# Masks ahead of scores, the second expert layer between halves of the first, and another order of the opening

## The chip, the cores and the metric

One core of a Trainium2 chip runs the kernel in one launch. The metric is the device time of that launch in microseconds (us). Three runs of the kernel before took 550.11, 551.80 and 550.82 us, median 550.82.

## The reference

A pre-norm block on x of 16 batches x 256 tokens x 128 features, all float32:

```python
x = x + attention(layernorm(x))   # 16 heads, d_k 8, d_v 64, causal softmax, then @ Wo
x = x + experts(layernorm(x))
# experts: probs = softmax(h @ gate_w) over 8 experts; each expert of each batch takes
# its top 64 of 256 tokens (top_k over tokens), y = gelu(xin @ w1) @ w2 with 512 hidden
# features, y *= top_p, and y is added back at the tokens' places
```

## The kernel before

**Attention.** Four heads of one batch are a unit `u = 4*b + j`; 64 units follow one another, and each engine runs the same software pipeline over them (`batches` calls `batch` per engine: batches -2 to 3 and 10 to 15 written out, the others in a hardware loop). All order is that of the instructions on each engine, with semaphores between engines. In one step, TensorE (PE) does: the second block's scores of unit u+1 into `s1_ps` (queries 128 to 255 against all 256 keys), the contexts of u-2 (L1075), once per batch extra work (transposed norms L1206, queries and keys L1034 to L1036, gate L1092), the transposes of the probabilities of u-1 (L1048, L1049), the output projection of u-3 (L1084), the last transposes (L1058), the values of u+2 (L1034 to L1036) and the first block's scores of u+2 into `s0_ps` (L1276). ScalarE (ACT) does the exponentials (L529) and half of the copies out of PSUM, VectorE (DVE) the row maxima (L939, L883), the other copies and the norms, GpSimd (POOL) the multiplication of the probabilities by their inverse sums (L482, L489). SyncE (SP) issues the transfers.

`s1_ps` is two banks, two heads in each. The scores are two matmuls on 64 rows of the array each (L1189, rows 0 to 63 for heads 0 and 1, rows 64 to 127 for heads 2 and 3; the queries are held as high and low parts in float32r, and 32 rows belong to a head). The causal mask is added by the array: four matmuls of bfloat16 tiles of 64 rows, 64 query columns by two heads (L1194). The whole step waits for `exp1`, the end of the exponentials of the block that the banks held before. A semaphore `s1_done` after the last of the six matmuls releases the row maximum.

**Opening.** `batch` with b = -2 and -1 fills the pipeline. There ACT clears the eight parts of the two key tiles (`zero_keys`, L522), four of them ahead of the first copy of transposed norms (L600); queries and keys are stored to DRAM and read back in the layout of the scores (SP L300, L328, L331), and the first unit's scores wait for that.

**Experts.** For n = 0 to 15, `n // 4` is a quarter of the batches and `n % 4` a pair of experts. PE runs `hidden(n, 0)` to `hidden(n, 3)` (L1146 to L1148, six matmuls of 256 columns each, 24 in all), `expert_out(n-1)` (L1162, 64 matmuls of 64 weight columns) and `out_product(n-5)` (L1172, eight matmuls, which put the rows of batch n-5 back at their tokens). `hidden` has two halves of a bank pair, `h_ps[k % 2]`: `hidden(n, k)` waits until ACT's gelu (L577) has read half k-2. `gather(b)` (L1125, four matmuls) fetches the tokens of batch b for the experts; `GATHERED_AT` and `GATHERED_AFTER` say at which n. ACT's `copy_xin` and DVE's `split_xin` turn it into `xin_hi` and `xin_lo`. DVE also builds the selection tiles (`picks` L830, `placing` L853), scales y (`scale_y` L875), finds the top tokens of batches 8 to 15 in 23 rounds (`top_round`, L790 to L796; one DMA round trip by `store_toks` and `load_toks` follows them) and adds the results (`add_out` L861, L864). y goes from L875 to ACT's L587 and POOL's L506, whose `y_lo_ready` `out_product` waits for.

## Time and profile before

| what | us |
|---|---|
| median of 3 runs | 550.82 |
| lowest, highest | 550.11, 551.80 |
| the profiled execution, its own time | 549.33 |
| its span in the trace | 547.60 |
| PE busy in the span | 517.3 (94%) |
| PE weight loads busy | 425.8 (78%) |
| DVE, ACT, POOL busy | 415.6, 405.0, 253.7 |
| mean granted clock of PE | 0.991 |

A matmul row begins when the matmul enters the array, and its length holds its way through the array too, so rows of one engine overlap; what a matmul costs is the distance from its start to the start of the next. PEld rows are the weight loads. The name after "<-" in brackets is what ended an engine's idle time.

### The profile page before, as it was taken

The numbers are of one execution on the slowest core, as the hardware profiler recorded it, in microseconds if no ns is written. First come the engines' busy times: TensorE is split into PE (matmuls) and PEld (weight loads), VectorE is DVE, ScalarE is ACT, GpSimd is POOL, SyncE is SP. The second block draws the span as 40 slices with busy tenths as digits, with TensorE's granted clock in tenths as the row PEclk, the third lists the DMA queues.
The fourth block names the chain that finished last, engine by engine and source line by source line (L and its number), as shares of the span: only waits on it lengthen the run. The fifth ranks groups of instructions, "written<-read, shape, count | busy, mean of one in ns | idle before, by whom it ended". The sixth has DMA issues, their size and how long they took to land.

```text
span 547.6 us, 13959 instructions
## 1 busy us (share of the span) xinstructions
PE 517.3 (94%) x4777; PEld 425.8 (78%) x4777; DVE 415.6 (76%) x1066; ACT 405.0 (74%) x1383; POOL 253.7 (46%) x249
## 2 busy tenths in 40 slices
PE   1489999999999999999999999999999999999996
PEld 1257777878878778787787877867789989899995
DVE  1477888888888888888999999999954876443354
ACT  4699999889998899988989889899555443424320
POOL 5165566565655655556555665556900110111011
PEclk9979999999999999999999999999999999999999
DMA  4576252742633325142251422502200012000011
GB/s 125 153 189 160 78 153 54 238 115 61 170 110 107 87 66 153 41 112 78 78 156 34 123 79 76 155 1 76 76 7 1 2 46 63 11 22 11 11 30 50
DMA packets 49783, 45.97 MB, mean 84 GB/s; under 512 B 4288, under 2 KB 46528, under 8 KB 49728
## 3 DMA queue, kind: packets, MB, share of 16 engines
q1 hardware_dynamic: 48864, 44.60, 29.9%
q8 instruction: 32, 0.52, 0.4%
q10 hardware_dynamic: 864, 0.66, 0.4%
q14 instruction: 23, 0.19, 0.1%
HBM read 26.35 MB, written 18.89 MB: 83 GB/s over the span
## 4 chain that ended last, share of the span: by engine, by line
PE 89%; ACT 4%; DVE 4%; issue 1%; DMA 1%; ACTq 0%; POOL 0%; DVEq 0%
PE ctx_ps L1075 16%; PE t_ps L1162 11%; PE misc_ps L1084 10%; PE t_ps L1048 5%; PE t_ps L1049 5%; PE s_ps L1189 5%; PE t_ps L1058 5%; PE misc_ps L1034 4%; PE s_ps L1146 4%; PE misc_ps L1036 3%; PE misc_ps L1035 3%; PE s_ps L1147 3%; PE s_ps L1148 3%; PE s_ps L1276 2%; PE ctx_ps L1172 2%; ACT prob L529 2%
## 5 line engine op out<-in xcount | busy, mean ns | idle before, releaser
L529 ACT ACTIVATE prob<-s_ps,neg_max 128x128 f32<-128x128 f32 (+1 forms) x512 | 208.4, 426 | 3.7 <-DVE neg_max L939 1.7
L489 POOL TENSOR_TENSOR probn<-prob,inv 128x1024 f32<-128x1024 f32 x64 | 121.2, 1893 | 54.7 <-DVE inv L960 54.7
L529 ACT ACTIVATION_READ_ACCUMULATOR prob<-s_ps,neg_max 128x1 f32 x512 | 108.4, 212 | 0.0
L482 POOL TENSOR_TENSOR probn<-prob,inv 128x512 f32<-128x512 f32 x64 | 66.6, 1040 | 67.3 <-PE t_ps L1058 59.0
L883 DVE TENSOR_REDUCE neg_max<-s_ps 128x4 f32<-128x1024 f32 x64 | 76.3, 1193 | 0.9 <-PE s_ps L1194 0.8
L506 POOL TENSOR_TENSOR y_parts<-y_sb,y_parts 128x512 fp32r<-128x512 f32 x16 | 20.6, 1286 | 112.7 <-ACT y_parts L587 112.7
L577 ACT ACTIVATE hT<-s_ps 128x512 f32<-128x512 f32 x64 | 38.0, 596 | 44.7 <-PE s_ps L1148 42.2
L1084 PE MATMUL misc_ps<-wo_sb,ctxT 128*128 128x128 f32 x512 | 67.8, 275 | 0.8 <-DVE x_all L708 0.8
L1084 PEld LDWEIGHTS misc_ps<-wo_sb,ctxT 128*128 128x128 f32 x512 | 62.2, 192 | 1.2 <-issue 1.2
L1048 PE MATMUL t_ps<-ident,probn 128*128 128x128 f32 x256 | 61.8, 281 | 0.0
L1049 PE MATMUL t_ps<-ident,probn 128*128 128x128 f32 x256 | 60.1, 275 | 0.0
L939 DVE TENSOR_REDUCE neg_max<-s_ps 128x4 f32<-128x512 f32 x64 | 44.2, 690 | 16.7 <-PE s_ps L1276 15.8
L538 ACT ACTIVATE probT<-t_ps 128x512 f32<-128x512 f32 x64 | 38.2, 597 | 18.9 <-PE t_ps L1049 18.0
L753 DVE COPY probT<-t_ps 128x512 f32<-128x512 f32 x64 | 44.1, 689 | 8.1 <-PE t_ps L1058 6.3
L1075 PE MATMUL ctx_ps<-probT,v_odd 128*64 128x256 f32 (+1 forms) x512 | 48.7, 332 | 0.8 <-ACT probT L543 0.7
L1075 PE MATMUL ctx_ps<-probT,v_even 128*64 128x256 f32 (+1 forms) x512 | 48.7, 332 | 0.7 <-DVE probT L753 0.5
L747 DVE COPY ctxT<-ctx_ps 128x512 f32<-128x512 f32 x64 | 43.5, 680 | 0.1
L1075 PEld LDWEIGHTS ctx_ps<-probT,v_odd 128*64 128x64 f32 x512 | 32.1, 136 | 14.0 <-ACT probT L543 1.2
L1075 PEld LDWEIGHTS ctx_ps<-probT,v_even 128*64 128x64 f32 x512 | 32.3, 136 | 13.0 <-issue 1.3
L892 DVE CAST s_ps<-causal 128x512 f32<-128x512 bf16 x63 | 42.4, 672 | 0.0
L1048 PEld LDWEIGHTS t_ps<-ident,probn 128*128 128x128 f32 x256 | 37.1, 145 | 3.9 <-issue 3.8
L543 ACT ACTIVATE probT<-t_ps 128x512 f32<-128x512 f32 x64 | 39.7, 620 | 0.0
(176 smaller groups left out, 1158.9 us busy)
## 6 DMA issues: line engine op xcount, KB each, us to landing
qT<-q_rows SPq DMA_DIRECT2D x15, 512.0 KB, 4.0
q_rows<-qk_hi SPq DMA_DIRECT2D x32, 128.0 KB, 2.4
q_rows<-qk_lo SPq DMA_DIRECT2D x32, 128.0 KB, 2.4
k_diag_odd<-k_rows SPq DMA_DIRECT2D x32, 128.0 KB, 4.2
k_rows<-qk_hi SPq DMA_DIRECT2D x30, 128.0 KB, 2.4
k_rows<-qk_lo SPq DMA_DIRECT2D x30, 128.0 KB, 2.4
k_diag_even<-k_rows SPq DMA_DIRECT2D x28, 128.0 KB, 4.2
w_raw<-in_L_ffn_w SPq DMA_DIRECT2D x1, 2048.0 KB, 9.8
```

Of the source, the lines that this page charges most:

```text
L482: nc.gpsimd.tensor_tensor(probn[r][:, 0:HG * P].rearrange("p (i k) -> p i k", i=HG), prob[r][:, 0:HG * P].rearrange("p (i k) -> p i k", i=HG),
L489: nc.gpsimd.tensor_tensor(probn[r][:, HG * P:].rearrange("p (i k) -> p i k", i=HG), prob[r][:, HG * P:].rearrange("p (i k) -> p i k", i=HG ...
L529: last = nc.scalar.activation(prob[r][:, first + i * keys:first + (i + 1) * keys], scores[:, i, :], ACT.Exp, bias=neg_max[:, r, block_, i: ...
L747: nc.vector.tensor_copy(ctxT[r][:, :, :], ctx_ps[:, :, :]).then_inc(ctx_ready, 1)
L753: nc.vector.tensor_copy(probT[rm][:, 1024:1536], t_ps[rm][:, :]).then_inc(t_dve, 1)
L883: nc.vector.tensor_reduce(out=neg_max[:, r1, 1, :], in_=s1_ps[:, :, :], axis=AX.X, op=ALU.max, negate=True).then_inc(max1, 1)
L939: nc.vector.tensor_reduce(out=neg_max[:, r2, 0, :], in_=s0_ps[:, :, :], axis=AX.X, op=ALU.max, negate=True).then_inc(max0, 1)
L1048: nc.tensor.transpose(t[:, i, 0:P], q0[:, 2 * f + i, :], ident[:, :])
L1049: last = nc.tensor.transpose(t[:, i, P:T], q1[:, 2 * f + i, 0:P], ident[:, :])
L1075: last = nc.tensor.matmul(ctx_ps[half * DV:(half + 1) * DV, pair, kb * P:T], v_sb[vb][:, kb, h * DV:(h + 1) * DV], rhs, start=(kb == 0), s ...
L1084: last = nc.tensor.matmul(misc_ps[1][:, tb * D:(tb + 1) * D], ctxT[r][:, c, tb * P:(tb + 1) * P], wo_sb[:, 2 * g + c, :], start=(g == 0 an ...
L1162: last = nc.tensor.matmul(y_ps[half * CAP:(half + 1) * CAP, q, :], hT[m % RING][:, half, c, q * CAP:(q + 1) * CAP], w2_of(2 * (m % EP) + h ...
```

## The change

1. `second_scores` puts the four mask matmuls ahead of the two score matmuls; the masks start the accumulation and the scores end it. The waits are the same.
2. In the expert stage PE runs `hidden(n, 0)`, `hidden(n, 1)`, `expert_out(n-1)`, `hidden(n, 2)`, `hidden(n, 3)`, then gathers, then `out_product(n-5)`, for each n. Batches 8 and 9 are gathered amid n = 7 in place of after n = 6. The gate product of batch 15 moves from the end of n = 1 into n = 2. DVE's work is reordered to go with it: the top rounds are split into parts ahead of and behind `scale_y` (`TOPS_AHEAD`, `TOPS_BEHIND`), `slots(1)` moves from n = 5 to n = 7, and the placing tiles of batches 12 to 15 lie in `xin_hi[0]` and `xin_lo[0]` (free once `hidden(11, 3)` is done) and are built at n = 12 to 15.
3. At the end `out_product` of batches 14 and 15 is done whole after the last y is ready; batches 12 and 13 still have three of four pairs ahead of it.
4. The opening is written out by hand for each engine, and the loop starts at b = 0. ACT clears two parts of the first key tile, after the first copy of transposed norms, and DVE the other six; the first norm comes ahead of the split of the weights; POOL computes both scales ahead of the mask tiles; two of the four first key loads are issued by ACT; both value products of the first tokens come ahead of the first scores.

```diff
-GATHERED_AFTER = {6: (8, 9), 7: (10, 11)}
+GATHERED_AMID = {7: (8, 9)}
+GATHERED_AFTER = {7: (10, 11)}
+TOPS_AHEAD = {4: range(6, 10), 5: range(15, 23)}
+TOPS_BEHIND = {3: range(0, 6), 4: range(10, 15)}
+LAST_PLACES_AT = 12
...
+            def second_scores(q, kb):
+                tiles = ((slice(0, HALF), 0), (slice(HALF, P), 2))
+                for half in range(2):
+                    cols = slice(P + half * HALF, P + (half + 1) * HALF)
+                    for rows, i in tiles:
+                        nc.tensor.matmul(s1_ps[:, i:i + 2, cols], half_rows[rows, half, :],
+                                         bcast(half_masks[rows, half, :], 1, 2),
+                                         start=(half == 0), stop=False, skip_group_check=True)
+                for rows, i in tiles:
+                    last = nc.tensor.matmul(s1_ps[:, i:i + 2, :], qT[kb][rows, q, P:T], k_diag[kb][rows, q, i:i + 2, :],
+                                            start=False, stop=True, skip_group_check=True)
+                last.then_inc(s1_done, 1)
...
+                for b in GATHERED_AMID.get(n, ()):
+                    gather(b)
+                if n == 2:
+                    pe.wait_ge(x2T_ready, B)
+                    gate(B - 1, side_ps)
+                if has(n - 1, B):
+                    expert_out(n - 1)
+                if has(n, B):
                     hidden(n, 2)
                     hidden(n, 3)
...
-            for b in range(LAST, B):
+            for b in range(LAST, B - 2):
                 out_product(b, range(EP - 1))
             pe.wait_ge(y_lo_ready, B)
-            for b in range(LAST, B):
+            for b in range(LAST, B - 2):
                 out_product(b, [EP - 1]).then_inc(out_done, 1)
+            for b in range(B - 2, B):
+                out_product(b, range(EP)).then_inc(out_done, 1)
```

The openings of ACT, DVE and PE in turn, which take the place of `batch` with b = -2 and -1:

```diff
+            split_norms(0, 0)
+            zero_keys(0, range(2))
+            split_qk(0)
+            act.wait_ge(qk_hi_done, 1)
+            store_rows(act, qk_hi, K_HI)
+            act.wait_ge(qk_lo_done, 1)
+            store_rows(act, qk_lo, K_LO)
+            act.wait_ge(wv_loaded, 16)
+            nc.scalar.activation(wv_hi[:, :], wv_raw[:, :], ACT.Copy).then_inc(w_hi, 1)
+            split_norms(1, 1)
+            act.wait_ge(qk_stored, QK_STORES)
+            act.wait_ge(zeroed, 3)
+            for i in range(2, HG):
+                act.dma_start(f32(k_diag[0][i * ROWS:(i + 1) * ROWS, 0:1, i, :]),
+                              k_rows.rearrange("(j i) r d t -> i (r d) j t", j=G)[i][:, 0:1, :]).then_inc(first_loaded, 16)
+            copy_values(0, 0, 0)
+            copy_values(1, 1, 0)
+            act.wait_ge(max0, 1)
+            exps(0, 0, s0_ps, P, 0, exp0)
+            split_qk(1)
+            act.wait_ge(max1, 1)
+            exps(0, 1, s1_ps, T, HG * P, exp1)
...
+            dve.wait_ge(x_loaded[0], 16)
+            norm_stats(lambda tb: x_all[:, tb, :], bn6, mv1, bn1_done, 1, stats1)
+            norm1(0)
+            split_qk_weights()
+            dve.wait_ge(x_loaded[1], 16)
+            norm_stats(lambda tb: x_all[:, TB + tb, :], bn6, mv1, bn1_done, 2, stats1)
+            split_norms(0, 0)
+            zero_keys(0, 2)
+            split_qk(0)
+            zero_keys(0, 3)
+            norm1(1)
+            zero_keys(1, 0)
+            dve.wait_ge(w_hi, 3)
+            nc.vector.tensor_tensor(wv_lo[:, :], wv_raw[:, :], f32(wv_hi[:, :]), ALU.subtract).then_inc(w_lo, 1)
+            split_norms(1, 1)
+            for j in range(1, G):
+                zero_keys(1, j)
+            dve.wait_ge(s0_done, 1)
+            nc.vector.tensor_reduce(out=neg_max[:, 0, 0, :], in_=s0_ps[:, :, :], axis=AX.X, op=ALU.max, negate=True).then_inc(max0, 1)
+            dve.wait_ge(s1_done, 1)
+            nc.vector.tensor_reduce(out=neg_max[:, 0, 1, :], in_=s1_ps[:, :, :], axis=AX.X, op=ALU.max, negate=True).then_inc(max1, 1)
+            dve.wait_ge(exp0, 1)
+            nc.vector.reciprocal(inv[:, 0, 0, :], sums[:, 0, 0, :]).then_inc(inv0, 1)
+            nc.vector.tensor_copy(s0_ps[:, :, :], bcast(causal[:, :], 1, HG)).then_inc(filled0, 1)
+            split_qk(1)
+            dve.wait_ge(s0_done, 2)
+            nc.vector.tensor_reduce(out=neg_max[:, 1, 0, :], in_=s0_ps[:, :, :], axis=AX.X, op=ALU.max, negate=True).then_inc(max0, 1)
+            dve.wait_ge(exp1, 1)
+            nc.vector.reciprocal(inv[:, 0, 1, :], sums[:, 0, 1, :]).then_inc(inv1, 1)
...
+            turn_first_norms(0)
+            pe.wait_ge(w_hi, 2)
+            pe.wait_ge(w_lo, 2)
+            pe.wait_ge(xT_ready, 1)
+            queries_keys(0)
+            nc.tensor.matmul(s0_ps[:, :, :], ident_bf[:, :], bcast(causal[:, :], 1, HG), start=True, stop=True)
+            pe.wait_ge(qk_lo_done, 1)
+            turn_first_norms(1)
+            pe.wait_ge(w_hi, 3)
+            pe.wait_ge(w_lo, 3)
+            pe.wait_ge(xT_ready, 2)
+            values(0, 0)
+            pe.wait_ge(v_ready, 1)
+            values(1, 0)
+            pe.wait_ge(v_ready, 2)
+            pe.wait_ge(first_loaded, QK_LOADS)
+            first_scores(0, 0)
+            pe.wait_ge(halves, 10)
+            second_scores(0, 0)
+            queries_keys(1)
+            pe.wait_ge(qk_loaded, QK_LOADS)
+            pe.wait_ge(filled0, 1)
+            first_scores(1, 0)
+            pe.wait_ge(qk_lo_done, 2)
```

## Rows read from the trace of the kernel before

**Rows 1.** The page: the chain that ended last, by engine.

```profile
PE 89%; ACT 4%; DVE 4%; issue 1%; DMA 1%; ACTq 0%; POOL 0%; DVEq 0%
```

**Rows 2.** Windows: span of window, busy us of each engine, granted clock, DMA.

```profile
30.00:35.00 5.00, 3.78 (x14) 1.96 (x14) 3.89 (x12) 4.90 (x24) 3.88 (x5) 0.50 0.50 142
...
100.00:200.00 100.00, 99.82 (x871) 79.84 (x870) 87.24 (x216) 90.77 (x348) 58.81 (x51) 1.00 0.45 127
```

**Rows 3.** Timeline, opening: start us, us, engine, line, operation.

```profile
6.59 3.87 ACT L522 ACTIVATE k_diag_even<-eps_sb 128x1024 fp32r<-128x1024 f32 x4
7.17 0.59 DVE L692 TENSOR_SCALAR xn<-x_all,mv,rstd 128x128 f32<-128x128 f32 x2
...
10.37 0.36 ACT L600 ACTIVATE xT_hi<-misc_ps 128x256 fp32r<-128x256 f32 x1
...
12.99 0.60 ACT L604 ACTIVATE qk_hi<-misc_ps 128x512 fp32r<-128x512 f32 x1 [2.26 <-PE misc_ps L1036]
...
19.23 0.35 SPq L328 DMA_DIRECT2D qT<-q_rows  x1
...
21.40 0.76 PE L1034 MATMUL misc_ps<-wv_hi,xT_hi 128*128 128x512 f32 x1 [1.02 <-DVE xT_lo L920]
...
28.99 0.49 PE L1189 MATMUL s_ps<-k_diag_even,qT 64*128 64x512 f32 x2
```

**Rows 4.** Timeline, two attention steps, PE and the exponential before each.

```profile
201.67 0.22 ACT L529 ACTIVATION_READ_ACCUMULATOR prob<-s_ps,neg_max 128x1 f32 x1
201.73 0.40 PE L1276 MATMUL s_ps<-k_diag_even,qT 128*128 128x512 f32 x1
...
202.06 0.49 PE L1189 MATMUL s_ps<-k_diag_even,qT 64*128 64x512 f32 x2
...
202.40 0.28 PE L1194 MATMUL s_ps<-half_masks,half_rows 64*128 64x128 bf16 x4
...
202.61 1.52 PE L1075 MATMUL ctx_ps<-probT,v_odd 128*64 128x256 f32 x16
...
207.83 0.23 ACT L529 ACTIVATION_READ_ACCUMULATOR prob<-s_ps,neg_max 128x1 f32 x1
...
208.11 0.50 PE L1189 MATMUL s_ps<-k_diag_even,qT 64*128 64x512 f32 x2
```

**Rows 5.** Timeline, first unit: a bfloat16 matmul, then a float32r one.

```profile
22.90 0.61 PE L1275 MATMUL s_ps<-causal,ident_bf 128*128 128x512 bf16 x1
22.91 0.31 PEld L1276 LDWEIGHTS s_ps<-k_diag_even,qT 128*128 128x128 f32 x1
...
23.87 0.79 PE L1189 MATMUL s_ps<-k_diag_even,qT 64*128 64x512 f32 x2
```

**Rows 6.** Waits: engine, line, waited for: us in total, times, longest.

```profile
PEld s_ps L1189 <- ACT prob L529: 23.2, 61, 0.7
```

**Rows 7.** Timeline, one turn of the expert stage on PE.

```profile
521.61 3.71 PE L1162 MATMUL t_ps<-w_first,hT 128*64 128x128 f32 x64
525.26 0.39 PE L1146 MATMUL s_ps<-xin_hi,w_hi 128*128 128x256 f32 x1
...
526.68 0.28 PE L1148 MATMUL s_ps<-xin_hi,w_lo 128*128 128x256 f32 x1
526.99 0.39 PE L1146 MATMUL s_ps<-xin_hi,w_hi 128*128 128x256 f32 x1
...
528.52 1.12 PE L1172 MATMUL ctx_ps<-y_parts,place 128*128 128x256 f32 x8
529.57 3.71 PE L1162 MATMUL t_ps<-w_rest,hT 128*64 128x128 f32 x64
```

**Rows 8.** Timeline, the end: last products, last addition.

```profile
538.01 0.98 PE L1172 MATMUL misc_ps<-y_parts,place 128*128 128x256 f32 x6
...
544.33 0.42 DVE L864 TENSOR_TENSOR x_all<-misc_ps,x_all 128x256 f32<-128x256 f32 x1
```

**Rows 9.** One line: count, min/median/max ns of one, first and last start.

```profile
L790 DVE MAX8 top<-left x16: 407/420/422, 289.2 to 441.7; 64x8 f32<-64x256 f32 x16
```

More of the change, by code:

```diff
@@ L188, in block_kernel @@
                                   t_ps[0][:, :], misc_ps[1][:, :])]
-        last_place = [part[:, :, :].rearrange("p t (a n) -> p (t a) n", a=2) for part in pick]
+        last_place = [half for part in (xin_hi[0], xin_lo[0]) for half in
+                      (part[:, 0:EP, :, :].rearrange("p e q s -> p e (q s)"),
+                       part[:, EP:E, :, :].rearrange("p e q s -> p e (q s)"))]
         def w2_of(e):
@@ L302, in batches @@
         def batches(engine, batch):
-            for b in range(-2, 4):
+            for b in range(4):
                 batch(b, b % 2)
@@ L517, in _, with zero_keys @@
                                      scale=(DK ** -0.5 if w == 0 else 1.0)).then_inc(w_hi, 1)
-            def zero_keys(r):
+            def zero_keys(r, groups):
                 act.wait_ge(consts, 4)
-                for j in range(G):
+                for j in groups:
                     last = nc.scalar.activation(k_diag[r][:, j, :, :].rearrange("p i t -> p (i t)"),
@@ L841, in split_xin, with take_gathered @@
                                         f32(xin_hi[b // QB % RING][:, :, b % QB, :]), ALU.subtract).then_inc(xin_lo_ready, 1)
+            def take_gathered(b):
+                if b + 1 not in (PASS, PASS + 3, PASS + 4) and b + 1 < B:
+                    picks(b + 1)
+                split_xin(b)
             def placing(b):
@@ L980, in _ @@
             for n in range(B + 2):
+                for b in GATHERED_AT.get(n, ()):
+                    take_gathered(b)
                 if n == 1:
@@ L1020, in _ @@
                     scale_y(m)
-                if n == 5:
+                if n == 1:
+                    copy_x2T(B - 1, side_ps)
+                if n == 3:
+                    copy_probs(1, side_ps[0:HALF, 0:T])
+                for s in TOPS_BEHIND.get(n, ()):
+                    top_round(1, s)
+                if n == 7:
+                    picks(PASS + 4)
+                for b in GATHERED_AFTER.get(n, ()):
+                    take_gathered(b)
+                if n == 6:
+                    picks(PASS)
                     picks(PASS + 1)
+                    placing(2)
                 b = n - 5
-                if has(b, LAST) and b % QB == 0:
+                if has(b, LAST):
                     add_out(b)
+                b = {4: -1, 5: 1}.get(n, n - 3)
+                if has(b, LAST):
+                    await_count(dve, out_done, b - 1)
+                    placing(b)
             for b in range(LAST, B):
@@ L1182, in batch @@
                     if has(u + 1, UNITS):
-                        q, kb = (j + 1) % G, par if j < 3 else 1 - par
-                        if isinstance(u, int) and u == -1:
-                            pe.wait_ge(halves, 10)
                         await_count(pe, exp1, u + 1)
-                        tiles = ((slice(0, HALF), 0), (slice(HALF, P), 2))
-                        for rows, i in tiles:
-                            nc.tensor.matmul(s1_ps[:, i:i + 2, :], qT[kb][rows, q, P:T], k_diag[kb][rows, q, i:i + 2, :],
-                                             start=True, stop=False, skip_group_check=True)
-                        for half in range(2):
-                            cols = slice(P + half * HALF, P + (half + 1) * HALF)
-                            for rows, i in tiles:
-                                last = nc.tensor.matmul(s1_ps[:, i:i + 2, cols], half_rows[rows, half, :],
-                                                        bcast(half_masks[rows, half, :], 1, 2),
-                                                        start=False, stop=(half == 1), skip_group_check=True)
-                        last.then_inc(s1_done, 1)
+                        second_scores((j + 1) % G, par if j < 3 else 1 - par)
                     if has(u - 2, UNITS):
@@ L1317, in _ @@
                     gather(b)
+                if n == 6:
+                    turn_tops(1)
                 if n == 3:
@@ L1324, in _ @@
                     turn_norms(B - 1, side_ps)
-                b, m = n - 5, n - 1
-                if b % QB == 0 and has(m, B):
-                    expert_out(m)
+                b = n - 5
                 if has(b, LAST):
@@ L1334, in _ @@
                     out_product(b, range(EP)).then_inc(out_done, 1)
-                if b % QB != 0 and has(m, B):
-                    expert_out(m)
-                if n == 1:
-                    pe.wait_ge(x2T_ready, B)
-                    gate(B - 1, side_ps)
-                if n == 5:
-                    turn_tops(1)
             pe.wait_ge(xin_hi_ready, B)
```

192 lines of the change are left out of this document (88 added, 104 removed).

## The prediction

> **What bounds the kernel now.** I read the page first. In its chain that ended last PE holds 89% and every other engine 4% or less [rows 1]: time taken from PE comes off the end. The windows then say where: from 100 to 200 us PE is busy for 99.82 of 100 us at a granted clock of 1.00, while DVE and ACT have 87.24 and 90.77 [rows 2]. But a busy PE row holds the way through the array, so the third view is the timeline of PE in one step, where the distance between starts is the cost. There three places show where PE gives time away: the opening, the switch to the second block's scores, and the break between the halves of the first expert layer. The change touches all three.
>
> **Opening.** It isn't PE-bound: a chain of single operations leads to the second unit's scores at 28.99 [rows 3]. The copy of the transposed norms starts at 10.37, since ACT has four clearings ahead of it (6.59 to 10.46), although the norm is written from 7.17 on [rows 3]. What follows hangs on it at fixed distances: queries and keys copied at 12.99, first key load issued at 19.23 (after the stores have landed), values at 21.40, first scores behind the masks at 22.90 [rows 3, 5].
> After the change the norm starts without waiting for the split of the weights, about 5.5 by my estimate, and ACT's copy follows at about 6.9. DVE then computes the second batch's statistics before it splits the norms, to about 8.5; PE's six matmuls start at 8.6, and ACT's copy of queries and keys at about 10.15 in place of 12.99: 2.85 us earlier. The two clearings left on ACT (3.87 / 4 = 0.97 each) lie under this. The stores and key loads keep their distance of 6.2 us (12.99 to 19.23): issue at 16.4, and two of the four issues go to ACT, so the keys are there at about 19.5.
> Now the values are late next: ACT issues its four stores, then splits the value weights (about 13.4 to 14.5), DVE splits them to 15.7 behind one clearing, and PE starts the values at 16.3. Two products, each followed by ACT's copy and a wait for it (21.40 + 0.76 for the first matmul of one, about 2.2 with its copy), end at 20.8. First scores then, against 22.95: 2.1 us earlier, and as ACT's exponentials of the first block no longer stand behind a late second block, I get the scores at 28.99 at about 26.1. DVE's six clearings cost 1.1 us each (my estimate; ACT's are 0.97), and four of them stand behind the first stores, where DVE waits anyway. POOL's mask tiles end about 4 us later, at 14.6, well before their first use at 21.4. I take 2.9 us. Bounds: the copy at 12.99 moves by at most 12.99 - 6.69 - 2.6 = 3.7; and 0.5 if DVE's clearings or the two value products take the place of what went. The clock comes in here: the trace has 0.50 (1.2 GHz) in the window 30 to 35 after a stretch with gaps [rows 2], and whether it still falls there moves about 1 us either way.
>
> **Masks ahead of scores.** 64 times; 60 of them where PE is the bound. The page's waits put 23.2 us of PE's weight loads before L1189 down to ACT's exponentials [rows 6], 0.37 each. The timeline corrects that: the last exponential ends at 201.67 + 0.22 = 201.89, and L1189 starts at 202.06, 0.17 later; at 208.11 it starts 0.05 after 207.83 + 0.23 [rows 4]. So 0.05 is what the semaphore needs, and in most steps something else sets the start: L1276 to L1189 is 0.33, where 512 columns at 2.4 GHz are 0.213. About 0.11 goes to the change from 128 rows to 64. The order of masks and scores doesn't touch that.
> What it touches is the 0.55 from 202.06 to 202.61. The score matmuls' rows are 0.49 long against 0.40 for L1276 [rows 4]: 0.095 of exposed weight load. So before: 0.095 load, 0.213 columns, 0.03 to the masks at 202.40, 0.12 for four masks of 128 columns, two at a time, and 0.09 to turn the array to L1075. The masks' own loads are bfloat16 and short (none of it visible before 202.40).
> After: masks first, 0.01 of load and 0.12 of columns. The score loads can start when the second pair of masks streams, at +0.08, and need 0.095: scores at +0.17, end of columns at +0.39, contexts at +0.48. Saved: 0.07 per unit, 60 x 0.07 = 4.2 us.
> For this the float32r load has to run under a bfloat16 matmul. Rows 5 show that it does: the load of L1276 starts at 22.91, 0.01 after the bfloat16 matmul L1275, and from 22.90 to 23.87 there are 0.97 us, which is two times 512 columns at 1.2 GHz (0.853) and the 0.11 of the turn: nothing is left for an exposed load. That is with 128 rows, though; in the masked tiles no row shows it. Bounds for the step: no overlap, 0.00 (load 0.095 still exposed, now between masks and scores); full overlap, 0.095 + 0.03 = 0.125, or 7.5 us. Below nothing: if each change between mask pairs and scores also drained the array at 0.11, two of them would make it 0.55 + 0.20. I take 0.07, nearest to rows 5 with the shorter cover of 128 columns.
> The Trainium skill speaks against me here: its page "TensorE: Matmul & The Clock Gate", section "Part 3: Packing small matmuls — row/col tiling", says that a weight load overlaps running matmuls only when it goes to another row group; the scores' loads go to the masks' own row groups. By it the step saves nothing (rival 1).
> Who follows? ACT's chain of a step starts from PE's transposes, so it moves along. Where ACT is busy from one step to the next, its slack before L1189 is 0.17 - 0.05 = 0.12 [rows 4], more than 0.07. s1_done comes 0.07 earlier too. In the last four units DVE sets the pace; they give nothing and are left out.
>
> **Expert stage.** One turn of n before: L1162 521.61 to 529.57 = 7.96 [rows 7]. In it the second half of `hidden` starts at 526.99, 0.31 after the last matmul at 526.68, where the spacing is 0.12: 0.19 of waiting for gelu; and its first matmul is 0.39 long against 0.28, 0.10 of exposed load: 0.29 in all. With L1162 (3.65) between the halves, gelu (0.6) is hidden. The array is still turned twice per n, once into L1162 and once out, as before. And `hidden(n+1, 0)` now follows `out_product`, whose 0.96 covers the gelu that it needs (it ends 0.2 + 0.6 after half 2, and half 3 alone takes 0.72). So 0.29 to 0.30 for each n from 5 to 15, and 0.1 more at n = 5, 9 and 13, where the old order put L1162 next to L1172 and cost a turn: 11 x 0.295 + 0.3 = 3.5. For n = 1 to 4 there is no `out_product`, the wait moves to the start of n: 0.5 from gathers that cover it, less 0.4 for `gate(14 + 1)`, which now waits for DVE behind ACT's last norm copy: about 0.1 (0 to 0.5). The gather of batch 9, which waited for its selection tile at n = 6, gives 0.3.
> **End.** `out_product(11)`, 529.57 - 528.52 = 1.05, stood ahead of the last L1162 and now stands behind it, in time in which PE had other products to do anyway. From L1162's end (538.01) the path is y through DVE, ACT and POOL, then DVE's eight additions until 544.33 + 0.42, then the store [rows 8]: PE isn't in it as long as it keeps ahead of DVE. With two products whole behind the last y it does: 0.48 and 1.92 after y against DVE's 0.8 per batch, the last product ends about 0.3 before DVE wants it. Gain 1.05. Adding up: 3.5 + 0.1 + 0.3 + 1.05 = 4.95, and 0.1 for the turn that `out_product(11)` paid: 5.05, say 5.1. Bounds 2.5 to 5.7.
> Hidden, and priced: the top rounds at 0.42 to 0.5 per operation [rows 9]. At n = 5 eight stand ahead of `scale_y(4)`, 4.0 us, plus 0.9 for `tops(1)`; I get `scale_y(4)` done 0.5 us before `expert_out(5)` wants it. Beyond that each us of DVE is a us of PE. After `hidden(7, 3)` the gathers 10 and 11, `out_product(2)` and gather 12 (3.75 us) cover the last split (3.4 us): 0.3 of slack. Moving `slots(1)` and `picks(8)` to n = 6 and 7 leaves about 3.5 us to the gather.
>
> **Sum.** The profiled execution took 549.33, 1.73 more than its span. 549.33 - 2.9 - 4.2 - 5.1 = 537.1. The median of the runs lies 1.49 above that execution: **538.6**.
>
> **Rivals.**
> 1. *The score loads stay exposed.* For: in the same tiles the masks' loads didn't start under the scores (202.40, after their columns). Against: rows 5. Masks ahead give 0: 549.33 - 8.0 = 541.3, or 542.8 as a median.
> 2. *A new wait takes part of it.* DVE's rounds ahead of `scale_y` stall `expert_out(4)` or `(5)`, or the gathers at n = 7 or 8 find their split late, by 1 to 2 us; or the opening gives 1 in place of 2.9. For: slacks of 0.3 and 0.5. Against: DVE has idle time at all other n. 541.
> 3. *Full overlap*, 0.12 per unit, with the opening as forecast: 535.5.
> 4. *Slower.* Each change between the mask pairs and the scores drains the array, as the change of rows does at 0.11: then masks ahead cost 0.20 x 60 = 12 us in place of saving, and 549.33 - 8.0 + 12 + 1.5 = 554.8. The point where this turns the sign is 8.0 / 60 = 0.133 per unit. Against: four masks lie in 0.21 with the turn behind them [rows 4], so pair to pair doesn't drain.
>
> **Numbers.** Forecast 0.50; rival 1 0.22; rival 2 0.12; rival 3 0.10; rival 4 0.04; the rest 0.02 for a change that is not seen. The forecast's own range is 537 to 540.5. To hold 8 in 10 I reach up over rival 1 and down to rival 3's edge: 534.5 to 544. What a measurement of this kernel tells from no change is about 0.3%, 1.65 us. Faster 0.94, same 0.02, slower 0.04.
>
> **What would show it.** In the opening: the scores now at 28.99 come at 26 to 26.5, queries and keys are copied at 10 to 10.5. In the units: the masks' first matmul to the contexts' first is 0.48 (forecast), 0.55 (rival 1), 0.43 (rival 3), 0.7 and more (rival 4); L1276 to the first of them stays 0.33; four units take 23.0 in place of 23.3 us. In the expert stage a turn without a gather takes 7.66 in place of 7.96, with no gap between the halves of `hidden`, and PE waits for y_sb nowhere at n = 4 to 8. At the end 9.6 us lie between the end of L1162 and the end of the span, as now. I am wrong if the units keep their 0.55, if PE waits for DVE between n = 4 and 8, or if the first 40 us give less than 1 us.

## The result, and the profile after

The changed kernel takes 540.79 us, median of 4 runs (539.42 to 541.56), against 551.11 for the kernel before (4 runs, 550.11 to 551.80): a ratio of 0.9826, 95% interval 0.9806 to 0.9845. It is faster by about 10 us. 538.6 was forecast, with 537 to 540.5 as the forecast's own range and 534.5 to 544.0 as the wide one: the measured time lies in the wide range and 0.3 above the narrow one. All ratios below are to runs of the kernel before that were taken together with each kernel, and leave out one run of 648.78 (`m_only`) and one of 846.33 (the kernel before beside it), which fell in a slower state of the chip with mean granted clocks of 0.76 and 0.57. The profiled execution took 540.85 with a span of 539.1, against 549.33 and 547.6 before: 8.5 apart, less than the medians, because the profiled execution of before was 1.8 under its median.

The chain that ended last, by engine, on the page of the kernel after; PE still holds most of it [rows 1]:

```profile
PE 87%; DVE 5%; ACT 3%; issue 2%; DMA 1%; ACTq 1%; POOLq 0%; POOL 0%; DVEq 0%
```

Windows of the kernel after, with the columns of [rows 2]: the middle is as full as it was, so time that PE saves there comes off the end, and the opening shows a clock of 1.00 throughout, which turns out to mislead.

```profile
5.00:10.00 5.00, 2.41 (x9) 1.79 (x9) 2.73 (x12) 2.88 (x6) 2.31 (x6) 1.00 0.66 174
...
30.00:35.00 5.00, 4.50 (x21) 3.57 (x21) 3.94 (x8) 4.82 (x23) 4.19 (x5) 1.00 0.59 173
...
100.00:200.00 100.00, 99.62 (x870) 79.63 (x868) 87.74 (x217) 91.71 (x348) 58.43 (x52) 1.00 0.45 124
```

Timeline of the opening of the kernel after (start us, us, engine, line, operation), against [rows 3]:

```profile
6.89 0.38 ACT L540 ACTIVATE xT_hi<-misc_ps 128x256 fp32r<-128x256 f32 x1 [0.50 <-PE misc_ps L1125]
...
9.02 0.41 PE L1117 MATMUL misc_ps<-xT_hi,wqk_hi 128*128 128x256 f32 x1
...
9.24 0.41 PE L1118 MATMUL misc_ps<-xT_lo,wqk_hi 128*128 128x256 f32 x1
...
9.90 0.60 ACT L546 ACTIVATE qk_hi<-misc_ps 128x512 fp32r<-128x512 f32 x1 [0.74 <-PE misc_ps L1119]
...
15.95 0.76 PE L1117 MATMUL misc_ps<-wv_hi,xT_hi 128*128 128x512 f32 x1 [2.75 <-DVE xT_lo L755]
...
21.31 0.40 PE L1153 MATMUL s_ps<-half_masks,half_rows 64*128 64x128 bf16 x4
...
26.42 0.40 PE L1153 MATMUL s_ps<-half_masks,half_rows 64*128 64x128 bf16 x4 [1.06 <-ACT prob L558]
```

The norm's copy starts 3.5 us earlier (6.89 for 10.37), queries and keys are copied at 9.90 (12.99), the values start at 15.95 (21.40) and the second unit's second block at 26.42 (28.99).

One attention step of the kernel after, PE and its weight loads, against [rows 4]:

```profile
199.24 0.40 PE L1144 MATMUL s_ps<-k_diag_even,qT 128*128 128x512 f32 x1
...
199.57 0.29 PE L1153 MATMUL s_ps<-half_masks,half_rows 64*128 64x128 bf16 x4
199.66 0.48 PE L1157 MATMUL s_ps<-k_diag_even,qT 64*128 64x512 f32 x2
200.07 1.52 PE L1198 MATMUL ctx_ps<-probT,v_odd 128*64 128x256 f32 x16
...
199.63 0.19 PEld L1157 LDWEIGHTS s_ps<-k_diag_even,qT 64*128 64x128 f32 x2
```

The scores' loads start at 199.63, when the second mask pair starts, and the scores at 199.66. From the first of the six matmuls to the contexts it is 0.506 in the median of the units, where it was 0.558.

One turn of the expert stage of the kernel after, against [rows 7]:

```profile
504.11 0.28 PE L1271 MATMUL s_ps<-xin_hi,w_lo 128*128 128x256 f32 x1
504.32 3.71 PE L1285 MATMUL t_ps<-w_first,hT 128*64 128x128 f32 x64
507.96 0.39 PE L1269 MATMUL s_ps<-xin_hi,w_hi 128*128 128x256 f32 x1
...
509.50 1.12 PE L1295 MATMUL ctx_ps<-y_parts,place 128*128 128x256 f32 x8
510.46 0.28 PE L1269 MATMUL s_ps<-xin_hi,w_hi 128*128 128x256 f32 x1
...
511.99 1.20 PE L1285 MATMUL t_ps<-w_first,hT 128*64 128x128 f32 x18
```

A turn is 511.99 - 504.32 = 7.67 where it was 7.96, and between L1295 and the next half nothing is left open (509.50 + 0.96 = 510.46).

The end of the kernel after, against [rows 8]:

```profile
529.54 1.22 PE L1295 MATMUL ctx_ps<-y_parts,place 128*128 128x256 f32 x8
...
532.48 0.51 PE L1295 MATMUL misc_ps<-y_parts,xin_hi 128*128 128x256 f32 x2 [0.28 <-POOL y_parts L517]
...
535.86 0.43 DVE L930 TENSOR_TENSOR x_all<-misc_ps,x_all 128x256 f32<-128x256 f32 x1
```

Batch 11's product now stands at 529.54, behind the last L1285. From the end of that L1285 to the end of the span it is 9.58 us, and it was 9.59 from the end of the last L1162.

For the comparisons below I follow marks through every trace: the first of the six matmuls of units 1 and 5 (the opening), of unit 59 (the PE-bound units lie between) and of unit 63, and the start of the last expert product.

| profiled execution | unit 1 | unit 5 | unit 59 - unit 5 | unit 63 to last product |
|---|---|---|---|---|
| before | 28.99 | 49.23 | 307.73 | 153.86 |
| after | 26.42 | 47.74 | 305.73 | 148.87 |

So in this pair the opening gave 1.49, the units 2.0, and everything behind them 4.99: together 8.48.

### The profile page after: what moved, and what is told of

It reads as the page before. It is cut to its first block, busy times and chain, and to the rows that moved or that the text cites. A ratio compares the mean times of both kernels' runs of the same rounds, so it can differ in the third digit from the quotient of the medians.

```text
span 539.1 us, 13960 instructions
## 1 busy us (share of the span) xinstructions
PE 514.4 (95%) x4777; PEld 424.5 (79%) x4777; DVE 420.4 (78%) x1072; ACT 401.1 (74%) x1377; POOL 258.4 (48%) x249
## 4 chain that ended last, share of the span: by engine, by line
PE 87%; DVE 5%; ACT 3%; issue 2%; DMA 1%; ACTq 1%; POOLq 0%; POOL 0%; DVEq 0%
PE ctx_ps L1198 16%; PE t_ps L1285 10%; PE misc_ps L1207 10%; PE t_ps L1171 5%; PE t_ps L1181 5%; PE t_ps L1172 5%; PE misc_ps L1117 4%; PE s_ps L1269 4%; PE misc_ps L1119 3%; PE misc_ps L1118 3%; PE s_ps L1157 3%; PE s_ps L1270 3%; PE s_ps L1271 3%; PE s_ps L1144 3%; PE s_ps L1153 2%
## 5 line engine op out<-in xcount | busy, mean ns | idle before, releaser
L949 DVE TENSOR_REDUCE neg_max<-s_ps 128x4 f32<-128x1024 f32 x63 | 75.2, 1194 | 1.7 <-PE s_ps L1157 1.6
L992 DVE TENSOR_REDUCE neg_max<-s_ps 128x4 f32<-128x512 f32 x62 | 42.9, 691 | 13.5 <-PE s_ps L1144 12.7
L1171 PEld LDWEIGHTS t_ps<-ident,probn 128*128 128x128 f32 x256 | 37.1, 145 | 4.3 <-issue 4.0
```

What stands on the lines that cost most here:

```text
L949: nc.vector.tensor_reduce(out=neg_max[:, r1, 1, :], in_=s1_ps[:, :, :], axis=AX.X, op=ALU.max, negate=True).then_inc(max1, 1)
L992: nc.vector.tensor_reduce(out=neg_max[:, r2, 0, :], in_=s0_ps[:, :, :], axis=AX.X, op=ALU.max, negate=True).then_inc(max0, 1)
L1171: nc.tensor.transpose(t[:, i, 0:P], q0[:, 2 * f + i, :], ident[:, :])
```

## The experiments

**One part of the change at a time.** From the kernel before, each of the three parts alone; the fourth kernel is the whole change without its masks. `m_only`:

```diff
                         tiles = ((slice(0, HALF), 0), (slice(HALF, P), 2))
-                        for rows, i in tiles:
-                            nc.tensor.matmul(s1_ps[:, i:i + 2, :], qT[kb][rows, q, P:T], k_diag[kb][rows, q, i:i + 2, :],
-                                             start=True, stop=False, skip_group_check=True)
                         for half in range(2):
@@ -1193,5 +1190,8 @@
                             for rows, i in tiles:
-                                last = nc.tensor.matmul(s1_ps[:, i:i + 2, cols], half_rows[rows, half, :],
-                                                        bcast(half_masks[rows, half, :], 1, 2),
-                                                        start=False, stop=(half == 1), skip_group_check=True)
+                                nc.tensor.matmul(s1_ps[:, i:i + 2, cols], half_rows[rows, half, :],
+                                                 bcast(half_masks[rows, half, :], 1, 2),
+                                                 start=(half == 0), stop=False, skip_group_check=True)
+                        for rows, i in tiles:
+                            last = nc.tensor.matmul(s1_ps[:, i:i + 2, :], qT[kb][rows, q, P:T], k_diag[kb][rows, q, i:i + 2, :],
+                                                    start=False, stop=True, skip_group_check=True)
                         last.then_inc(s1_done, 1)
```

> The kernel before with only the masks put ahead of the scores. Theory: the step from the first of the six matmuls to the contexts falls from about 0.556 to 0.506 us, PE gets 0.045 us in three units of four and nothing in the fourth, where the contexts wait for ACT's copy: 2.0 to 2.3 us in all, about 549 against 551. Rival (the prediction's price of 0.07 per unit, of which other steps of the change took a part): 4 us, about 547. Rival (the whole gain depends on the new opening): nothing.

Measured: 547.47 median (12 runs) against 550.0 (23 runs), ratio 0.9952 (0.9937 to 0.9967), 2.6 us with an interval of 1.8 to 3.5. Unit 59 - unit 5: 305.65, against 307.73, so 2.1 us there; the step from the masks to the contexts 0.506. Both rivals are out; what the text says of the fourth unit is put right below. Its opening was slow in the profiled execution (unit 5 at 50.28), which is why the unit distances tell more than the spans.

`x_only`: the expert stage alone, as in the diff of the change.

```diff
                 if has(n, B):
                     hidden(n, 0)
                     hidden(n, 1)
+                if has(n - 1, B):
+                    expert_out(n - 1)
+                if has(n, B):
                     hidden(n, 2)
                     hidden(n, 3)
...
```

> The kernel before with only the new order of the expert stage and of the end. Theory: 5.0 us less, 546, turns of 7.66 to 7.67 us without a gather against 7.96. Rival (part of the 5.0 comes from the attention stage arriving earlier and its DVE work being done earlier): under 4 us.

Measured: 544.67 (6 runs), ratio 0.9901 (0.9875 to 0.9927), 5.4 us. Unit 63 to the last product takes 148.70 (before: 153.86), and a turn without a gather 7.67, so it doesn't need the other two parts.

`o_only`: the opening alone.

```diff
-            for b in range(-2, 4):
+            for b in range(4):
                 batch(b, b % 2)
...
+            split_norms(0, 0)
+            zero_keys(0, range(2))
+            split_qk(0)
...
```

> The kernel before with only the new opening. Theory: the second unit's scores start about 2.6 us earlier, but the gain that reaches the fifth unit depends on when the granted clock rises to 2.4 GHz, so 1.5 to 2.6 us less, 549. Rival (the opening's 2.6 us stay whole): 2.6 to 3 us in every run. Rival (DVE's clearings and the value products eat it): under 1 us.

Measured: 548.01 (12 runs), ratio 0.9961 (0.9947 to 0.9976), 2.1 us. Unit 1 at 26.47, unit 5 at 47.86. Of the 2.5 us that unit 1 gains, not all arrives, as the theory had it.

`no_m`: the kernel after with the scores ahead of the masks again.

```diff
                 tiles = ((slice(0, HALF), 0), (slice(HALF, P), 2))
+                for rows, i in tiles:
+                    nc.tensor.matmul(s1_ps[:, i:i + 2, :], qT[kb][rows, q, P:T], k_diag[kb][rows, q, i:i + 2, :],
+                                     start=True, stop=False, skip_group_check=True)
                 for half in range(2):
@@ -1152,8 +1155,5 @@
                     for rows, i in tiles:
-                        nc.tensor.matmul(s1_ps[:, i:i + 2, cols], half_rows[rows, half, :],
-                                         bcast(half_masks[rows, half, :], 1, 2),
-                                         start=(half == 0), stop=False, skip_group_check=True)
-                for rows, i in tiles:
-                    last = nc.tensor.matmul(s1_ps[:, i:i + 2, :], qT[kb][rows, q, P:T], k_diag[kb][rows, q, i:i + 2, :],
-                                            start=False, stop=True, skip_group_check=True)
+                        last = nc.tensor.matmul(s1_ps[:, i:i + 2, cols], half_rows[rows, half, :],
+                                                bcast(half_masks[rows, half, :], 1, 2),
+                                                start=False, stop=(half == 1), skip_group_check=True)
                 last.then_inc(s1_done, 1)
```

> The changed kernel with the masks behind the scores again. Theory: 2.0 to 2.3 us slower than the changed kernel, with units of 23.3 us per batch in place of 23.15; 543. Rival (0.07 per unit): 4 us slower, 545.

Measured: 542.83 (6 runs), ratio 0.9867 (0.9842 to 0.9893), 2.3 us less gained than by the whole change; unit 59 - unit 5 back at 307.72. The timeline of `no_m` in the step that answers to the one above shows where: the scores are 0.50 long with their load exposed, and the masks start 0.35 behind them.

```profile
200.27 0.39 PE L1144 MATMUL s_ps<-k_diag_even,qT 128*128 128x512 f32 x1
200.59 0.50 PE L1151 MATMUL s_ps<-k_diag_even,qT 64*128 64x512 f32 x2
200.94 0.29 PE L1156 MATMUL s_ps<-half_masks,half_rows 64*128 64x128 bf16 x4
201.15 1.52 PE L1198 MATMUL ctx_ps<-probT,v_odd 128*64 128x256 f32 x16
```

The parts add up: 2.6 + 5.4 + 2.1 = 10.1 by the ratios against 9.6 for the whole. The intervals are about 1 us wide on each side, so a part that lives on another by more than some 2 us is ruled out, and a smaller overlap isn't.

**A longer cover.** `cover` puts the second mask pair in twice, to see whether the exposed rest of the scores' load goes when more bfloat16 work stands ahead of it (the columns of these matmuls are keys, so the last 64 keys get their mask twice).

```diff
-                for half in range(2):
+                for half in (0, 1, 1):
```

> The changed kernel with the second pair of mask matmuls issued twice (those mask values are added twice). Theory: a weight load starts only when the matmul pair before it starts, so the scores' loads get no more cover from a third pair, their exposed part stays 0.08, and the step grows by a pair, 0.067, from 0.506 to 0.573 us. Rival (loads can run ahead of more than one pair, and only the cover was short): the step grows by 0.02 or less. Rival (a load doesn't overlap matmuls in its own row group at all): exposed 0.095 already, the step grows by 0.067 as well but the scores' rows are 0.49 long, not 0.48.

Measured in one run: 544.8; unit 59 - unit 5 307.77, the step to the contexts 0.555, 0.049 more than after. The timeline of `cover`:

```profile
201.11 0.34 PE L1153 MATMUL s_ps<-half_masks,half_rows 64*128 64x128 bf16 x6
201.26 0.47 PE L1157 MATMUL s_ps<-k_diag_even,qT 64*128 64x512 f32 x2
201.67 1.52 PE L1198 MATMUL ctx_ps<-probT,v_odd 128*64 128x256 f32 x16
...
201.24 0.19 PEld L1157 LDWEIGHTS s_ps<-k_diag_even,qT 64*128 64x128 f32 x2
```

The load starts at 201.24, together with the last mask pair and not with the one before it. So it runs ahead by one pair here, as the theory had it, and a third pair hides little more of it: the scores' row is 0.471 long, 0.477 after. The step grew by less than the theory's 0.067, since a further pair takes 0.055 and not 0.067 (the pairs start at 201.11, 201.18 and 201.24). `cover` also lost 1.4 us between unit 63 and the first expert product. Its trace has PE wait there for 1.46 us for ACT's copy of the turned probabilities (0.73 in the kernel after) and for 0.63 for DVE's; why those come later is open.

**The same two kernels again**, since the profiled pair differed by less than the medians.

> The kernel before once more, for a second trace. Theory: the attention steps and the expert turns have the same lengths to 0.01 us, and what differs from the first trace (whose execution was 1.5 us under the median) lies in the first 45 us, where the granted clock rises and falls at other times. Rival: the difference is spread over the whole span.

> The changed kernel once more. Theory: the second unit's scores again at 26.4 us, the fifth unit's between 41 and 42 by where the clock rises; all later lengths the same.

Measured: 549.2 and 540.0, one run each. The second has unit 1 at 26.41 and unit 4, the fifth in that text's count, at 41.01. Unit 5 comes at 48.84 and 47.02; behind it both repeat the first pair to 0.1 us (307.79 and 305.70 from unit 5 to unit 59). What differs from execution to execution lies ahead of unit 5. With the old opening unit 5 came at 48.84, 49.23, 50.28 (`m_only`) and 51.27 (`x_only`), in the order in which the granted clock rose to 1.0 for good: 35.3, 36.4, 38.6 and 40.4 us. With the new one it came at 47.02, 47.16, 47.74, 47.76, 47.86 and 48.25. The means, 49.9 and 47.6, are 2.3 apart. With the new opening the rise lay between 35.2 and 37.1, in nearly the same order. Three of the four old openings also show a stretch at 1.0 before that, which no trace of the new opening has: 26.2 to 29.6 in `before`, one more in `before_again` and two in `m_only`. From unit 1 to unit 5 those three took 20.24 to 20.52, `x_only`, without such a stretch, 21.69, and the six traces of the new opening 20.61 to 21.54.

**The clock of the opening.** `warm` puts 40 bfloat16 matmuls of 512 columns into PE's waits of the opening; they write to a PSUM tile that is not in use yet, and nothing of the result depends on them.

```diff
+FILL = (7, 3, 8, 10, 2, 3, 5)
+            def filler(count):
+                for _ in range(count):
+                    nc.tensor.matmul(ctx_ps[:, :, :], ident_bf[:, :], bcast(causal[:, :], 1, HG), start=True, stop=True)
...
+            filler(FILL[0])
             turn_first_norms(0)
+            filler(FILL[1])
...
             queries_keys(0)
...
+            filler(FILL[2])
             pe.wait_ge(qk_lo_done, 1)
             turn_first_norms(1)
+            filler(FILL[3])
...
             values(0, 0)
+            filler(FILL[4])
             pe.wait_ge(v_ready, 1)
             values(1, 0)
+            filler(FILL[4])
...
```

> The changed kernel with 41 idle-time matmuls (bfloat16, 512 columns, into the contexts' bank, whose value nobody reads) in PE's waits of the opening. Theory: the missing 1.1 us between the third and fifth unit and more of the opening is PE at 1.2 GHz; kept busy, PE is granted 2.4 GHz before the first values, the value products and scores halve, and the fifth unit's scores come 1.5 to 3.5 us earlier: about 538. Rival (the opening hangs on ACT, DVE and transfers, and PE's clock costs nothing there): no change. Rival (the added matmuls stand in the way): slower by up to 2 us.

(They are 40, not 41: the fifth count is used twice.) Measured: 537.04 (5 runs, 536.77 to 538.3), ratio 0.9764 (0.9742 to 0.9786), unit 5 at 44.23, so neither rival holds. Once more, with its fillers unchanged, and with only the first four groups of them (28 matmuls, `FILL = (7, 3, 8, 10, 0, 0, 0)`):

> The kernel with all 40 bfloat16 matmuls in the waits of the opening once more, unchanged. It tells how far its profile repeats. If the clock is what makes the first 45 us differ from execution to execution, the first scores of unit 5 come at 44.2 within 0.3 again, where they lay from 47.0 to 48.3 in the others with the new opening, and the time is 536.8 to 537.4. If the 3.5 us were luck of one execution, they come at 46 or later. The last store landed about 1 us later in that execution than in the others, against the start of the last output product: if that is chance, the span ends about 9.8 after the last expert product starts, not 10.8, and the span is 535.6.

> The kernel with bfloat16 matmuls put into PE's waits of the opening, but only in the first four of them (28 matmuls, up to the values); the last 12 (before and behind the second value product, before the second unit's scores and before the units) are left out. Their results are overwritten, as before. Theory A: the granted clock stays up once it has risen as long as the gaps are short, and the gaps behind the values (up to some 3 us with PE busy 3.5 of 5 us) let it fall again, as it does in the kernel before after 29.6 us: clock 1.0 from about 6, back to 0.5 at some point from 20 to 33, first scores of unit 5 at 45 to 47, time 538 to 539.5. Theory B: what matters is only that it rises early; then it stays at 1.0 and the time is the one of the kernel with all fillers, 537.0, within 0.5.

Measured: `warm_again` 537.23 (4 runs, 536.96 to 537.28), ratio 0.9747 (0.9726 to 0.9769), unit 5 at 43.80 and a last store on time, so the late one was chance. `warm_half` 537.8 (4 runs, 537.55 to 538.01), ratio 0.9760 (0.9739 to 0.9782), unit 5 at 44.66. The timeline of `warm_again` has the query and key products 0.12 apart where the kernel after has them 0.21 apart, at 9.02 and 9.24 above:

```profile
8.94 0.28 PE L1118 MATMUL misc_ps<-xT_hi,wqk_hi 128*128 128x256 f32 x1
9.06 0.28 PE L1119 MATMUL misc_ps<-xT_lo,wqk_hi 128*128 128x256 f32 x1
```

Both windows show a granted clock of 1.00 there. In the kernel after that isn't the clock but the absence of a record before its first change: 256 columns in 0.21 are 1.2 GHz, and the clock's first record in that trace is the rise at 36.83. `warm_half` shows what the last fillers are for (windows, with the clock in the third column from the right):

```profile
15.00:20.00 5.00, 3.44 (x16) 2.02 (x17) 2.92 (x6) 1.47 (x4) 3.06 (x8) 0.96 0.65 184
20.00:25.00 5.00, 2.97 (x13) 1.79 (x12) 3.29 (x7) 4.84 (x24) 2.20 (x2) 0.50 0.38 107
25.00:30.00 5.00, 4.08 (x16) 2.32 (x16) 4.09 (x12) 4.12 (x20) 3.34 (x5) 0.50 0.49 134
30.00:35.00 5.00, 5.00 (x32) 3.39 (x32) 3.76 (x9) 4.28 (x16) 2.92 (x3) 0.67 1.02 250
```

Without them the clock falls back at 19.6 and returns at 33.3; in `warm_again` it is 1.00 in all windows up to 50. Theory A was right on that and wrong on its price. Unit 0 comes at 18.90 (after: 21.31), 2.4 us of the gain; from unit 1 to unit 5 it takes 20.97, against 21.32 after and 19.74 in `warm_again`. So most of the gain is made ahead of the first scores. The fall costs 1.2 us from unit 1 to unit 5; 0.9 of it is left at unit 5, since unit 0 comes 0.36 earlier than in `warm_again` (19.26). By the medians `warm_half` and `warm_again` are 0.6 apart, with intervals that overlap.

**The move between the halves by itself.** `whole` is the kernel after with the second layer's product behind all four parts of the first.

```diff
-                if has(n - 1, B):
-                    expert_out(n - 1)
                 if has(n, B):
                     hidden(n, 2)
                     hidden(n, 3)
+                if has(n - 1, B):
+                    expert_out(n - 1)
```

> The kernel after with one move undone in the expert stage: the product of the second expert layer stands again behind all four parts of the first layer, instead of between its halves. Everything else of the change stays (batch 11's output product behind the last expert product, the new order of DVE's rounds, batch 8 and 9 gathered amid the halves, the new opening, masks ahead of scores). Theory: the interleaving alone gives what the trace of before showed between the halves, 0.19 of waiting for gelu and 0.10 of exposed load, so a turn without a gather goes from 7.67 back to 7.96 with a gap of 0.31 between the halves; 11 to 15 such turns cost 3.2 to 4.4 us, and the time rises by 3.2 to 4.5 us, a ratio of about 0.990 to the kernel before. Rival: most of the 5.1 us of the expert stage came from the rest (the end, the turn of the array saved at batch boundaries, the gathers); then a turn stays under 7.8 and the time rises by less than 1.5 us, a ratio under 0.985.

Measured: 543.38 (4 runs, 543.02 to 544.48), ratio 0.9867 (0.9842 to 0.9891). By the ratios 2.3 us of the 9.6 are lost, less than the theory's 3.2 and more than the rival's 1.5. From unit 63 to the last product it takes 151.70: 2.83 more than after, 2.16 less than before. The timeline of `whole` has the gap of [rows 7] again, 505.77 - 505.46 = 0.31, and a turn of 515.36 - 507.40 = 7.96:

```profile
505.46 0.28 PE L1271 MATMUL s_ps<-xin_hi,w_lo 128*128 128x256 f32 x1
505.77 0.38 PE L1269 MATMUL s_ps<-xin_hi,w_hi 128*128 128x256 f32 x1
...
507.40 3.71 PE L1285 MATMUL t_ps<-w_first,hT 128*64 128x128 f32 x64
511.04 1.22 PE L1295 MATMUL ctx_ps<-y_parts,place 128*128 128x256 f32 x8
...
515.36 3.71 PE L1285 MATMUL t_ps<-w_first,hT 128*64 128x128 f32 x64
```

The place of the gap and its 0.29 are as the theory had them. The sum in the trace is a little under its 3.2, since at n = 6 `whole` was 0.2 faster than after (9.77 for 9.97).

## Why the prediction was right, and where it was off

- **Bound and sum.** What PE saved came off the end, and the three parts add within their intervals. The sum promised 12.2 us and 9.6 came (by the ratio): the expert stage gave what was forecast, and the masks and the opening fell short. So the time is within the range although two of its three terms are too large. At 541 it is also what rival 2 forecast, and only the traces tell the two apart.
- **Expert stage and end, 5.1.** Measured 4.99 in the profiled pair, 5.4 by `x_only`. A turn is 7.67, forecast 7.66; no gap; the traces name no wait of PE for `y_sb`; the end keeps its 9.6. `whole` splits it: 2.8 for the place between the halves, 2.2 for the rest (1.05 of it batch 11's product by the prediction's argument; no run has it by itself). Nor does PE wait for DVE's rounds: from 405 to 530 the trace has no wait of a matmul, and none of a weight load over 0.4. So the first branch of rival 2, DVE in the way, did not come.
- **Opening, 2.9.** The order was right, and each step was 0.1 to 0.4 earlier than forecast: the copy at 9.90 (10.15), the value weights split from 13.15 (13.4), values at 15.95 (16.3), first scores at 20.59 (20.8). One estimate was far off: DVE's clearings take 0.68 to 0.74, where I put 1.1. Yet unit 1 came at 26.42, forecast 26.1, because the exponentials of the first unit's second block, which the scores wait for (1.06 in the row above), now end last. 2.57 us were gained there. By unit 5 it was 1.49 in this pair, 2.3 in the mean of the executions, and 2.1 by `o_only`, where I took 2.9. That is part of the way to rival 2's second branch, an opening that gives 1. The step that was off is the last one, "I get the scores at about 26.1" and nothing given back behind it: PE has no gap in the timeline from 31.50 to the rise of the clock at 36.83 and runs at 1.2 GHz there, and when the rise comes varies from execution to execution by more than the error. `warm` shows that this clock has a price: with it up from 6.26, unit 1 to unit 5 takes 19.72.
- **Masks, 4.2.** The mechanism was right and the term mis-sized: 2.0 by the profiled pair, 2.6 by `m_only`, 2.3 by `no_m`. The loads of the scores do run under the second mask pair, in the same row groups. The columns started at +0.17, as forecast (the row starts at +0.095, and 0.08 of its 0.477 is beyond the 0.40 that a row without exposed load has). The masks' columns end at about +0.12 (0.067 to the second pair and 0.055 for it, as in `cover`), so by my estimate from these rows about 0.05 of the load is left uncovered, where 0.095 was. What the sum had too low is the turn to the contexts: I took it at 0.09, as it was behind the masks, and it is 0.506 - 0.17 - 0.213 = 0.12 behind the scores. The step shrank by 0.050 in the mean and not by 0.07, and from one unit to the next 0.044 of it arrived.
  Then there are units that give nothing. Of the 54 from unit 5 to unit 59, 46 give 0.034 to 0.054 each, 2.04 together, and eight give -0.04 together: 2.0, what was measured. What the text of `m_only` says, nothing in every fourth unit, isn't so. The eight are units 17, 21, 25, 29, 33 and 37, the second unit of each batch that runs in the hardware loop, and units 44 and 58; the same unit of the batches that are written out (9, 13, 41, 45, 49, 53, 57) saves 0.037 to 0.054. In the six the step itself is longer and doesn't shrink (0.719 and 0.716 in unit 29, 0.676 and 0.677 in unit 33). What holds the contexts there isn't shown. Unit 29 in the kernel before, then after:

```profile
184.97 0.63 ACT L543 ACTIVATE probT<-t_ps 128x512 f32<-128x512 f32 x1
185.16 0.50 PE L1189 MATMUL s_ps<-k_diag_odd,qT 64*128 64x512 f32 x2
...
185.88 0.87 PE L1075 MATMUL ctx_ps<-probT,v_even 128*64 128x256 f32 x8
```

```profile
182.57 0.63 ACT L572 ACTIVATE probT<-t_ps 128x512 f32<-128x512 f32 x1
182.76 0.28 PE L1153 MATMUL s_ps<-half_masks,half_rows 64*128 64x128 bf16 x4
...
183.48 0.76 PE L1198 MATMUL ctx_ps<-probT,v_even 128*64 128x256 f32 x6
```

  ACT's last copy of the turned probabilities (the first row) ends at 185.60 and 183.20, and the contexts start 0.28 behind it both times; over the six it is 0.24 to 0.28 in both kernels. That would fit contexts that wait for this copy. But in units 30 and 41 of the kernel after they start only 0.10 and 0.07 behind the same copy, and in the six they also stand at a fixed 0.72 to 0.77 behind the exponentials that release the step, so PE's own issuing in the loop would fit as well, and the view of the waits calls these idle times "issue". No run moved one without the other. In units 44 and 58 the step does shrink (0.558 to 0.506 in unit 44) and the next unit comes no earlier; that is open. My test of who follows looked only at ACT's slack before the second scores (0.12) and not at what stands before the contexts. The "23.0 in place of 23.3" for four units was too high on both sides: unit 5 to unit 59 makes 22.80 before and 22.65 after.
- **Rival 1** is out: at 0.55 the step would not have moved. The Trainium skill ("TensorE: Matmul & The Clock Gate", "Part 3: Packing small matmuls — row/col tiling") has in its list of what overlaps that a weight load does so only when it goes to another row group, and names the background weight buffer as a second way a few lines above. These rows disagree with the list, with a load at 199.63 into the row groups of the mask pair that starts then, and 0.17 from the first mask to the scores' columns. **Rival 3** is out too, since about 0.05 of the load stays uncovered, and so is **rival 4**: the scores' row starts 0.03 behind the second mask pair. Most of the 2.2 us between 538.6 and 540.79 is the masks' term, the rest the opening's.
- **What stays open.** Cover is not all that a load needs. In the kernel before, the masks' own loads started at 202.40, 0.33 behind the scores' matmuls, and didn't run under them, though each had 512 columns ahead of it; in both kernels the first load of the contexts starts only with its own matmul, behind bfloat16 masks (before) as behind float32r scores (after). No run here tries what decides whether the next load may start early.

## What to carry to other kernels

Ask of each matmul what stands right ahead of it. Here a short bfloat16 pair hid about half of the next one's float32r load, and a second pair ahead of it hid no more; the other order, bfloat16 behind float32r, hid nothing. So try both orders. When a step is shortened, go through all that its last instruction and the next group wait for, unit by unit, since a saving of 0.05 was worth nothing in eight units of 54. Add up the distances from unit to unit before dividing a total: here 2.0 us also fits a wrong count of units with a wrong saving. In an opening of chained small products, look at the distance between rows and not at the clock's column: matmuls that do nothing, put into the waits, brought the ratio to the kernel before from 0.9826 to 0.9764 and 0.9747 (540.79 to 537.04 and 537.23 us).

## What the runs showed of the hardware

- A float32r load for a 64-row tile ran under bfloat16 matmuls of the same rows. It made the score row 0.08 longer with two mask pairs ahead (`after`), 0.074 with three (`cover`), and 0.095 to 0.10 with none (`before`, `no_m`). It started with the pair right ahead of it each time.
- Behind the float32r score pair on 64 rows no load ran ahead: the masks' loads started 0.33 behind its start (202.40 and 202.06 in `before`).
- From the end of the columns to the contexts' 64-column tiles it took 0.12 behind 512 columns of float32r (`after`) and 0.09 behind 128 columns of bfloat16 (`before`). The contexts' own first load may be in it; the rows don't part the two.
- The clock was at 1.2 GHz up to its first record in every trace without fillers (256 columns in 0.21 for queries and keys), although the windows show 1.00 there. It rose at 6.26 us in `warm` and stayed, and fell in `warm_half` at 19.6 after a stretch in which PE was busy for 3.44 of 5 us. Executions with the same opening differed by up to 2.4 us at unit 5, in the order of that rise.
- DVE cleared 128x1024 float32 in 0.68 to 0.74; ACT took 3.87 for four.
